# A mixed-attention block with experts on one core: where the causal mask of the hyperbolic heads is applied

## What is computed

```python
inner = einsum('bhtd,bhsd->bhts', q, k) - tq * swapaxes(tk, -1, -2)
arg = maximum(-curv * inner, 1.0 + 1e-07)
dis = sqrt(1.0 / curv) * arccosh(arg)
scores = 1.0 / (eps + dis) + causal_bias        # -inf where key > query
y = softmax(scores) @ v
```

## Time and profile before

| | us |
|---|---|
| three runs | 2038.44, 2035.73, 2028.61 |
| median of the runs | 2035.73 |
| the profiled execution | 2027.79 |
| its span, first to last instruction | 2026.2 |

### The profile page before, as it was taken

The page is one execution under the profiler, slowest core; times in us unless marked ns, Lnnn a source line. Parts: engine busy times, 40 slices in busy tenths (PEclk is TensorE's granted clock), DMA queues, the critical chain, the costliest instruction groups (busy, mean ns, idle before and its releaser), DMA issues. The chain is left out here.

```text
span 2026.2 us, 38980 instructions
## 1 busy us (share of the span) xinstructions
PE 1621.9 (80%) x13082; PEld 912.6 (45%) x13082; DVE 1194.5 (59%) x3014; ACT 1391.7 (69%) x1456; POOL 820.5 (40%) x497
## 2 busy tenths in 40 slices
PE   7999858878976997798689778978977997618993
PEld 4665513334433443444334334434433443418993
DVE  5886746536854776576568567765865775421113
ACT  3665648887886888788778878888887888401110
POOL 3334424344443544544444445445444655300003
PEclk9999969889987998899799889978997998759997
DMA  4699731451065015505420650254055101149862
GB/s 163 199 246 293 224 107 52 88 91 34 2 106 117 12 18 92 116 12 74 112 49 2 105 117 12 31 90 114 2 85 126 47 21 43 43 160 413 319 239 73
DMA packets 66079, 215.18 MB, mean 106 GB/s; under 512 B 16944, under 2 KB 26800, under 8 KB 57104
## 3 DMA queue, kind: packets, MB, share of 16 engines
q1 hardware_dynamic: 56704, 179.35, 34.7%
q0 software_dynamic: 9200, 33.43, 5.3%
HBM read 144.14 MB, written 68.58 MB: 105 GB/s over the span
## 5 line engine op out<-in xcount | busy, mean ns | idle before, releaser
L1153 ACT ACTIVATE a_PT<-a_s 128x1024 f32<-128x1024 f32 (+3 forms) x576 | 460.0, 809 | 177.8 <-PE a_s L972 110.0
L969 PE MATMUL a_s<-Q,K 96*128 96x512 bf16 (+7 forms) x1152 | 331.4, 352 | 101.3 <-ACT a_PT L1153 71.9
L1231 POOL TENSOR_TENSOR a_Z<-a_Z,a_R 128x2182 f32<-128x2182 f32 x64 | 290.2, 4535 | 147.5 <-ACT a_R L1165 147.3
L1228 POOL TENSOR_TENSOR a_R<-a_Z 128x2182 f32<-128x2182 f32 x64 | 245.0, 3829 | 257.0 <-DVE a_Z L1350 192.4
L1358 DVE TENSOR_REDUCE a_mx<-a_w 128x1 f32<-128x512 f32 (+2 forms) x576 | 307.7, 550 | 55.9 <-PE a_w L997 42.5
L984 PE MATMUL a_o<-a_PT,a_V 128*32 128x512 f32 (+3 forms) x2304 | 268.7, 541 | 75.7 <-ACT a_PT L1153 46.8
L1350 DVE TENSOR_SCALAR_CACHE_REDUCE a_Z<-a_w 128x512 f32<-128x512 f32 (+7 forms) x384 | 202.3, 529 | 133.7 <-PE a_w L1012 94.1
L1029 PE MATMUL a_w<-a_ident,a_R 128*128 128x128 f32 (+1 forms) x1152 | 208.8, 309 | 19.0 <-POOL a_R L1238 7.7
L1404 DVE COPY a_PTh<-a_w 128x512 f32<-128x512 f32 (+1 forms) x256 | 157.6, 620 | 106.4 <-PE a_w L1029 101.9
L997 PE MATMUL a_w<-K,Q 96*128 96x512 bf16 (+2 forms) x576 | 187.7, 334 | 31.1 <-DVE a_mx L1358 9.7
L969 PEld LDWEIGHTS a_s<-Q,K 99*128 99x128 bf16 (+1 forms) x1152 | 112.1, 103 | 196.0 <-ACT a_PT L1153 109.2
(11 more groups left out here) (165 smaller groups left out, 2575.6 us busy)
## 6 DMA issues: line engine op xcount, KB each, us to landing
e_w<-in_w SPq DMA_DIRECT2D x23, 2048.0 KB, 8.7
qk_parts<-p_parts SPq DMA_DIRECT2D x128, 192.0 KB, 3.3
Q<-qk_parts SPq DMA_DIRECT2D x144, 128.0 KB, 5.3
K<-qk_parts SPq DMA_DIRECT2D x144, 128.0 KB, 7.1
v_rows<-p_vt SPq DMA_DIRECT2D x8, 2048.0 KB, 9.7
a_V<-v_rows SPq DMA_DIRECT2D x32, 512.0 KB, 8.7
p_xT<-in_xt SPq DMA_DIRECT2D x8, 1024.0 KB, 8.2
a_X<-in_x POOLq DMA_DIRECT2D x8, 1024.0 KB, 16.3
```

Source lines behind the costliest of these rows:

```text
L969: m = pe.matmul(sB[x % 2][:, i, 0:w], Kb[0:r, h, P * j:P * j + P], Qb[0:r, h, t0:t0 + w], start=True, stop=not diag)
L1153: act.activation(PT[:, u % 2, 2 * k:2 * k + 2, 0:w], sB[x % 2][:, :, 0:w], ACT.Exp, scale=scale_of(GROUPS[g][2 * k])).then_inc(prob.sem, 1)
L1228: pool.tensor_tensor(r, z, z, ALU.mult).then_inc(z_sq.sem, 1)
L1231: pool.tensor_tensor(z, z, r, ALU.add).then_inc(z_sum.sem, 1)
```

## The change

GpSimd's `mask` step is gone from the list, with its semaphore. The first transpose of a part waits for the second of its two exponentials instead. The copy of the diagonal block out of PSUM becomes a multiplication of that block by a 0/1 table in SBUF (keys down the partitions, queries along the row, repeated over the four heads). The table `hmasks[:, 1]` is rebuilt for that layout. All transposes stand one slot earlier, and `hyp_values` one slot later.

```diff
-            for part, masked, turned in ((0, 23, 28), (1, 28, 33)):
-                put(ready + masked, ("mask", n, part))
+            for part, turned in ((0, 27), (1, 32)):
                 for q in range(len(turns(n, part))):
                     put(ready + turned + q, ("turn", n, part, q))
             if n % 2:
                 for part in range(2):
-                    put(ready + 37 + part, ("hyp_values", HYP_TILES[n - 1 + part]))
+                    put(ready + 38 + part, ("hyp_values", HYP_TILES[n - 1 + part]))
...
                 if q == 0:
-                    pe.wait_ge(h_masked.sem, h_masked.at(d, 2 * n + part))
+                    pe.wait_ge(h_prob.sem, h_prob.at(d, 4 * n + 2 * part + 1))
...
-                elif kind == "mask":
-                    part = item[2]
-                    g, _, at, _ = segments(n)[2 * part]
-                    w = GK * (g + 1)
-                    pool.wait_ge(h_prob.sem, h_prob.at(d, 4 * n + 2 * part + 1))
-                    edge = R[:, n % RB, at:at + 2 * w].rearrange("p (f s) -> p f s", f=2)[:, :, w - GK:w]
-                    pool.tensor_tensor(edge, edge, hmasks[:, 1], ALU.mult).then_inc(h_masked.sem, 1)
...
-                    ins = dve.tensor_copy(PTh[0:w, NT - 1 + part, :, o:o + GK],
-                                          bank[0:w, a:a + 2 * P].rearrange("p (h t) -> p h t", h=N_HYP))
+                    allowed = hmasks[0:w, 1, g % 2, :].unsqueeze(1).to_broadcast([w, N_HYP, GK])
+                    ins = dve.tensor_tensor(PTh[0:w, NT - 1 + part, :, o:o + GK],
+                                            bank[0:w, a:a + 2 * P].rearrange("p (h t) -> p h t", h=N_HYP), allowed, ALU.mult)
...
-    hmasks = np.stack([np.where(ahead, 1e9, 0.0), ~ahead], 1).astype(np.float32)
+    allowed = np.arange(P)[:, None, None] <= 64 * np.arange(2)[None, :, None] + np.arange(64)[None, None, :]
+    hmasks = np.stack([np.where(ahead, 1e9, 0.0), allowed], 1).astype(np.float32)
```

More of the change, by code:

```diff
@@ L890, in attend @@
         b_ready = ev("a_b_ready", NU)
-        h_prob, h_masked = ev("a_h_prob", 4 * NU), ev("a_h_masked", 2 * NU)
+        h_prob = ev("a_h_prob", 4 * NU)
         y_inv, stats = ev("a_y_inv", NT), ev("a_stats", 4 * NT)
```

## The result

| | before | after |
|---|---|---|
| median of four runs, us | 2034.54 | 2007.87 |
| lowest and highest, us | 2028.61, 2038.44 | 2003.78, 2011.00 |
| the profiled execution, us (span) | 2027.79 (2026.2) | 2006.02 (2004.4) |
| ratio, 95% interval | 1 | 0.9878 [0.9846, 0.9909] |

The change makes the kernel 1.2% faster, 26.7 us between the medians. The forecast was 2030.6 us with a range of 2020 to 2042: right in sign, and far too small. Of the kernel after, first the engines' busy time on the page, then a group by line (columns as in the earlier trace rows), then that line's own view (shortest, median and longest in ns, first and last start).

The account below looks back on a forecast made before the run. No engine is full: TensorE and ScalarE wait for each other in turn. Batches -4.6, multiplication +0.5 and tail -1.0 sum to -5.1 us: 2022.7 against the profiled execution, 2030.6 against the median, range 2020 to 2042.

Parts of the forecast that it names:

- The mask off the path: Inside the batches no transpose waits for GpSimd's mask, so removing its 68.1 us of work is worth 0 there.
- The multiplication: VectorE's multiplication replacing the copy costs 13 ns more, 128 times; bounds 0 and +1.7 us, taken +0.5.
- Rival 4: GpSimd's long steps stop VectorE's multiplication: 100 us on VectorE, perhaps half showing, 2085 us; chance 0.03.
- Slots 27 to 32: Earlier transpose fills TensorE's wait in 27.2, 0.65 us off scores of 28.0; up to 0.85 us a batch, seven batches.
- The same move, slots 32.3 and 33.0: Unit 5's last transpose and copy now precede the second normalize, delaying the chain behind: +0.4 to +0.6 us a batch.
- The batch's end: Unit 6's first transpose runs inside the 6.24 us wait, 0.96 us off; long keys' rows waits swallow gains after slot 33.0.
- `hyp_values` at 0: Moving hyp_values a slot later, behind a pair of scores: 0, with 0.2 us either way for each of four tile pairs.
- The tail: After the last batch, transposes no longer wait for masks, 2.5 us sooner, less lower clock; bounds -2.5 and +1.4, taken -1.0.
- Rival 3: The waits for the keys' rows at batch boundaries get short, up to 20 us; half and the forecast give 2020; chance 0.14.

Follow-up runs that it names:

- e1: Kernel before with the multiplication in place of the copy and the mask gone, transposes and hyp_values in their old slots: 2028.63 us, ratio 0.9978.
- e2: Kernel before with transposes one slot earlier and hyp_values one later, GpSimd's mask step kept: 2031.7 us, ratio 1.0004.
- e17: Kernel after with rows_in two slots later, second group's loads held, and a plain copy for the multiplication, mask left out: 1979.51 us, ratio 0.9736.
- e13: Kernel before with both boundary edits: rows_in two slots later, SyncE's second group of loads held until the batch's first argument: 2008.38 us, ratio 0.9892.
- e16: Kernel after with rows_in later and second group's loads held, part 0's transposes back at slot 28: 2011.90 us, ratio 0.9905 to before.
- e15: Kernel after with rows_in later and second group's loads held, part 1's transposes back at slot 33: 1980.23 us, ratio 0.9754 to before.
- e11: Kernel after with both boundary edits: rows_in two slots later, second group's loads held until the batch's first argument: 1978.79 us, ratio 0.9755 to before.
- e8: Kernel after with only part 0's transposes earlier (27), part 1's back at 33, hyp_values back at +37, no boundary edits: ratio 0.9973 to before.
- e18: Kernel after with rows_in later and second group's loads held, part 1's transposes back at 33, hyp_values at +37: 1987.30 us, ratio 0.9778 to before.
- e14: Kernel after with rows_in later and second group's loads held, hyp_values back at +37: 1982.87 us, ratio 0.9769 to before.
- e7b: Kernel after with SyncE's loads of the second group of heads held until the batch's first argument: 1999.79 us, ratio 0.9855 to before.

## Why the prediction was wrong

- **The mask off the path: right for the old order** (e1), and this is where the argument stopped too early. It was a statement on the order of before. In the order that the change brings, TensorE waits 49.4 us for the mask, and the time is where it was (e2). I costed the removal and the move each on its own; they belong to one sum.
- **The multiplication: right.** Taken +0.5 us, bounds 0 and 1.7; the rows give 128 x 2 ns = 0.3 us, e17 nothing that can be told. Rival 4 did not happen.
- **"Slots 27 to 32": mis-sized, and for another reason than the one given.** I took 0.65 us off the scores of 28.0, the length of the wait that a transpose would fill, and called 0.85 us a batch the most. Slots 27 to 28 gave 1.33 in the mean, slots 28 to 30 took 0.23 back: 1.10 net. At one clock the move is worth 0 (down) to 0.9 us (up); the rest is that the clock is up in 21 batches of 36 where it was up in 6. The transposes behind the wait run at half the clock in most batches of before, 1.11 and 1.09 us in e13 (the earlier trace rows has the wait; the rows behind it I had read only for what fills it). I had the clock in the sum for the batch's end and for the tail, and not here. What I counted for `sums` and `normalize` did not show.
- **Slots 4 to 27 were at nothing, without a reason: a step that failed.** The same three numbers move the transposes of all eight units. I looked at the units around slot 27, and the others brought 0.36 + 0.19 us a batch. A moved step has to be costed at each of its places.
- **"The same move, slots 32.3 and 33.0": the loss did not come, a step that failed.** Taken +0.4 to +0.6; slots 31 to 35 measured -0.28 + 0.13 = -0.15, so seven batches came out 4.6 us better than the +0.5 that I took. Part 1 earlier does cost something there when it is alone (e16: 11.6 us for slots 31 to 33, 10.8 in e15), but not beside part 0.
- **The batch's end.** I took 0.96 us, one item of four transposes. The trace of after, at the boundary ahead of batch 6, the one of the earlier trace rows, shows six products instead of eight, not four: unit 6's first item left the place behind that wait, and its third, of two transposes, moved in from the slot behind:

```profile
1360.97 1.49 PE L1028 MATMUL a_w<-a_ident,a_R 128*128 128x128 f32 x6
```

  1.49 for 1.92 us, 0.43 off, as the quiet boundaries from batch 1 on say (21.2 in e13, 20.8 in e11). That the waits at the boundary would swallow what comes from above was the other half of this step, and for the change as a whole it failed too. Over the quiet boundaries of the same order, before lost 179.1 - 148.2 = 30.9 us and after 171.1 - 144.7 = 26.4. The gain from inside came through whole there. For part 0 alone it did not: e8 is 0.3% faster than before, where e18 is 0.6% faster than e13 less its 9 us. My reading, not tried by itself: SyncE's and GpSimd's transfers start from the work and move with it, so a saving ahead of them can be kept.
- **`hyp_values` at 0: the sign was missed.** One slot later took them from in front of a pair of scores to behind it. 4 to 7 us, shown only as a tendency (e14 and e11, e18 and e15).
- **The tail: mis-sized.** -1.0 taken, -3.0 measured, past the bound of -2.5. The rows of after: the transposes of unit 6, part 1 run in front of GpSimd's bias addition and not behind it, the exponentials of unit 7 start 14.4 us after slot 35.0 (16.4 before, and 14.4 in e1 too, so the removed mask does it), and eighteen transposes run straight through.

```profile
1721.62 2.13 PE L1028 MATMUL a_w<-a_ident,a_R 128*128 128x128 f32 x9
...
1724.46 4.54 POOL L1252 TENSOR_TENSOR a_X<-a_X,a_bias 128x2048 f32<-128x2048 f32 x1
...
1731.15 2.67 ACT L1179 ACTIVATE a_R<-a_R,a_nb 128x576 f32<-128x576 f32 x4 [0.29 <-DVE a_nb L1378]
1732.64 3.50 PE L1028 MATMUL a_w<-a_ident,a_R 128*128 128x128 f32 x18 [3.98 <-ACT a_R L1179]
```

```profile
1732.00:1736.50 4.50, 3.86 (x34) 3.62 (x38) 2.82 (x6) 1.81 (x3) 0.00 (x0) 0.62 0.00 0
```

  The mechanism was as forecast, and so was the lower clock behind the stand (0.62); but not the 1.5 us that I set against the gain: 2.0 of the 3.0 us were there when the exponentials began, and 1.0 more came behind them.
- **Rival 3 (the boundary waits get short)** happened in small: 4.5 us less of it at the boundaries, from one trace of each kernel. Its cause, more than one transfer in the way, was there in both kernels and was worth 26 to 31 us at the boundaries once both were out of it; the change does not remove it.

The sum as measured, per change: inside about -13 (forecast -2.5, 7 x -0.35), boundaries -3.5 from the order and about -4.5 from their waits (forecast -2.1 in all), tail -3.0 (-1.0), multiplication 0 (+0.5). That is 24 us, against 21.8 between the profiled executions and 26.7 between the medians. Of the 19 us that the forecast of 5.1 is short of this, the boundaries are 5.9, the loss in slots 32.3 and 33.0 that did not come 4.6, the slots 4 to 27 3.9, the tail 2.0 and slots 27 to 32 1.8: no one term carries the miss. The three largest are a wait that I let swallow the gain, a loss that did not come, and places that I left out.

**What stays open.** Why the clock falls in slot 25.2 in some batches and in 27 in others of the same kernel: the wait in front is 2.29 us both times. So the 1.7 and the 3.31 of the table can't be told ahead, and with them 2.7 us a batch (14.0 against 16.7 for slots 27 to 30), nor why the new order meets the first case more often. The gain of slots 4 to 27 was seen in all traces with part 0 at 27 and the mask gone, in batches of either clock, but not followed to one wait. The kernel of e1 with both boundary edits, which would be the base for the parts without the mask, was not run.

## What to carry to other kernels

A step that waits for nobody in one order may be what forbids a better order: cost a removal together with the move that it allows, since each alone can be worth nothing (0.9978 and 1.0004 against 0.9878). When a step is moved out from behind a wait of TensorE, look at the clock of the rows behind that wait over many batches and not in one, and price the step at every place of its list where it recurs. And where a boundary scatters from batch to batch, look for all transfers and queue heads that meet there: two holds that bring 0.05% and 0.2% alone brought 1.2% together on the kernel after, and only the quiet boundary let the parts of the change be told apart. The fastest kernel of this study is e11, the change with both holds: 1978.79 us.

## What the runs showed of the hardware

- TensorE's granted clock was halved behind a stand of 1.73 us in e13 (the transposes at 1115.80 take 1.11 us, where e15 has 0.66 at 1.00; 0.50 over the window that follows), and the same stand of 2.29 us is followed by 1.00 in one batch and 0.57 in the next of one execution.
- Transfers are held up by others that are issued after them: with the second group's loads, issued behind the keys' rows, held back, TensorE's waits for these rows fell from 27.0 to 2.9 us; to issue the rows ahead of the large blocks of their own group changed nothing (0.9997).
- The same slots of the same kernel take 14.0 or 16.7 us (slots 27 to 30), by whether TensorE's clock is granted at 1.00 or 0.50 at their start.
- A DMA issue of 0.94 us at the head of GpSimd's queue, which waits for a store to land, held the engine for 6.85 us; in e7b the addition queued behind it was ready 3.0 us before it started.
